# Summing runs of ten edges on VectorE before the products of sums on TensorE

## The reference, cut to what matters

```python
msg_in = concat([h[src], h[dst], edge_attr])          # 206250 x 160, h = relu(layernorm(x))
messages = silu(msg_in @ W1 + b1) @ W2 + b2           # 64 wide
att_logits = silu(msg_in @ Wa1 + ba1) @ Wa2 + ba2     # one number per edge
att = softmax(att_logits, axis=0)                     # over all edges
aggregated = segment_sum(messages * att, dst, 6250)
x + silu(concat([h, aggregated]) @ Wu1 + bu1) @ Wu2 + bu2
```

## Time and profile before

| | |
|---|---|
| timed runs, median | 2107.86 us |
| profiled execution, span | 2482.0 us |
| mean granted TensorE clock | 0.668 |
| busy: GpSimd | 1529.9 us (62%) |
| busy: TensorE matmul | 1101.1 us (44%) |
| busy: VectorE | 1086.6 us (44%) |
| busy: ScalarE | 919.5 us (37%) |
| mean DMA share of 16 engines | 18.5% + 17.2% in the two large queues |

### The profile page before, as it was taken

How to read it: one execution, slowest core, us unless ns; L and a number is a source line. 1 busy time by engine, 2 the same in 40 slices (tenths; PEclk the granted TensorE clock), 3 DMA queues, 4 the chain that set the end, 5 groups by cost and what they waited for, 6 DMA issues and landing times.

```text
span 2482.0 us, 21022 instructions
## 1 busy us (share of the span) xinstructions
PE 1101.1 (44%) x6767; PEld 963.4 (39%) x6767; DVE 1086.6 (44%) x2367; ACT 919.5 (37%) x1107; POOL 1529.9 (62%) x1628
## 2 busy tenths in 40 slices
PE   4334444444444444444444444444444444444447
PEld 3223343444333333444333334343433333444444
DVE  4344444444444444444444444444444444444445
ACT  3333333334333333334333333343433333333433
POOL 4666666666666666666666666666666666666650
PEclk8566666666666666666666666666666666666766
DMA  7433333333333333333333333333333333333321
GB/s 202 106 90 90 90 89 88 92 91 95 98 93 88 90 88 88 90 93 90 99 95 89 89 90 89 87 94 89 98 95 91 89 90 90 87 93 90 95 65 27
DMA packets 101990, 228.43 MB, mean 92 GB/s; under 512 B 45184, under 2 KB 65460, under 8 KB 91636
## 3 DMA queue, kind: packets, MB, share of 16 engines
q1 hardware_dynamic: 47588, 120.63, 18.5%
q0 software_dynamic: 51584, 105.75, 17.2%
q10 hardware_dynamic: 2704, 0.66, 0.1%
HBM read 218.91 MB, written 8.00 MB: 91 GB/s over the span
## 4 chain that ended last, share of the span: by engine, by line
issue 48%; PE 33%; DVE 9%; another core or an unknown queue 7%; ACT 1%; SPq 1%; DVEq 0%; DMA 0%; ACTq 0%
PE bank L622 20%; PE bank L636 11%; DVE hot L865 2%; DVE v L902 2%; DVE bank L912 1%; DVE prod L895 1%; PE bank L732 1%; PE bank L722 0%; DVE lgb L921 0%; DVEq L875 0%; ACT comb L492 0%; PE bank L584 0%; ACT s L524 0%; PE bank L655 0%
## 5 line engine op out<-in xcount | busy, mean ns | idle before, releaser
L404 POOL DMA_INDIRECT p_rows<-p_tab,src_all x1612 | 1521.9, 944 | 872.3 <-issue 464.7
L622 PE MATMUL bank<-q_win,comb 128*128 128x128 f32 x3224 | 723.7, 369 | 981.9 <-issue 963.8
L622 PEld LDWEIGHTS bank<-q_win,comb 128*128 128x128 f32 x3224 | 643.9, 279 | 1099.1 <-issue 1095.4
L492 ACT ACTIVATE comb<-dst_b,row_of 96x1024 f32<-96x1024 int32 (+1 forms) x162 | 219.0, 1352 | 1336.6 <-PE bank L622 1227.8
L911 DVE TENSOR_TENSOR bank<-bank,p_rows 128x128 f32<-128x128 f32 x80 | 23.9, 299 | 1205.5 <-remote 672.6
L636 PE MATMUL bank<-hot,v 128*65 128x96 f32 x3200 | 320.1, 252 | 344.7 <-issue 274.8
L636 PEld LDWEIGHTS bank<-hot,v 128*65 128x65 f32 x3200 | 282.7, 141 | 342.1 <-issue 264.5
L912 DVE TENSOR_TENSOR bank<-bank,p_rows 128x512 f32<-128x512 f32 (+1 forms) x403 | 266.5, 666 | 71.7 <-PE bank L622 38.6
L524 ACT ACTIVATE s<-bank 128x512 f32<-128x512 f32 x403 | 232.1, 589 | 108.7 <-DVE bank L912 83.8
L498 ACT ACTIVATE comb<-comb,ones 96x1024 f32<-96x1024 f32 (+1 forms) x162 | 218.9, 1351 | 2.7
L865 DVE TENSOR_TENSOR hot<-bank,rel 128x960 f32<-128x960 f32 x162 | 178.3, 1139 | 0.0
(11 more groups left out here) (108 smaller groups left out, 304.0 us busy)
## 6 DMA issues: line engine op xcount, KB each, us to landing
dst_b<-dst_row SPq DMA_DIRECT2D x80, 960.0 KB
p_rows<-p_tab,src_all POOLq DMA_INDIRECT x1612
comb<-efT SPq DMA_DIRECT2D x80, 320.0 KB
q_win<-q_tab SPq DMA_DIRECT2D x81, 48.0 KB
p_tab<-s SPq DMA_DIRECT2D x12, 256.0 KB
q_tab<-s SPq DMA_DIRECT2D x12, 256.0 KB
out<-s SPq DMA_DIRECT2D x6, 256.0 KB, 2.3
x_sb<-x SPq DMA_DIRECT2D x2, 512.0 KB, 5.1
```

The costliest lines, as they stand in the source:

```text
L404: pool.indirect_dma_start(p_rows[:, a, t * H2:(t + 1) * H2], None, p_tab, bass.IndirectOffsetOnAxis(src_all[:, g * TG + t:g * TG + t + 1], ...
L492: nc.scalar.activation(comb[0:WIN, a, c0:c1], dst_b[:, c0:c1], ACT.Abs, bias=row_of[0:WIN, bass.ds(g, 1)]).then_inc(abs_ok, 1)
L622: last = nc.tensor.matmul(ps_z[q][:, (t % TQ) * H2:(t % TQ + 1) * H2], comb[:, a, t * P:(t + 1) * P], q_win[:, a, :], start=True, stop=True)
```

## The change

The host lays the edges out differently: in a group, partition p now holds 20 consecutive edges instead of each 128th. Ten consecutive edges of one partition are a run (RUNS = 2 per group and partition; six edges in the last group). As edges are sorted by receiver, a run is taken to have at most two receivers, the first edge's and the last edge's. worst_fit checks this and keeps in first_run which edges have the receiver of their run's first edge.

Per group, VectorE splits the weights in two (w_run: those of first_run, and the others), multiplies s by each (the first product overwrites the logits' half of s2, the second goes to v), and adds up each over the ten edges of a run into run_sum: 4 columns of 65. One-hots are only needed for the first and last edge of each run, 4 tiles of 96. TensorE then has 4 products instead of 20. They stand behind all five quarters of the next z. The last group does the same, and its total weight is computed ahead of its sums.

```diff
+        first_run = sb("first_run", [P, C // P])
+        fits = sb("fits", [P, C // P])
+        hot = sb("hot", [P, SEGS * WIN])
+        w_run = sb("w_run", [P, 2, TG])
+        run_sum = sb("run_sum", [P, SEGS, U1])
...
             def sums(g):
-                pe.wait_ge(v_ok, g + 1)
-                pe.wait_ge(hot_ok, 2 * g + 2)
+                pe.wait_ge(hot_ok, g + 1)
                 wait(pe, acc_ok, g)
+                pe.wait_ge(run_ok, 2 * g + 2)
...
-                for t in range(T):
-                    last = nc.tensor.matmul(ps_part[0:U1, 0:WIN], v[:, t, :], hot[:, t * WIN:(t + 1) * WIN], start=(t == 0), stop=(t == T - 1))
+                for i in range(SEGS):
+                    last = nc.tensor.matmul(ps_part[0:U1, 0:WIN], run_sum[:, i, :], hot[:, i * WIN:(i + 1) * WIN], start=(i == 0), stop=(i == SEGS - 1))
                 last.then_inc(part_done, 1)
...
-                for q in [q for q in (0,) if q in quarters]:
-                    zmm(nxt, 1 - a, q)
-                for q in [q for q in (1, 2) if q in quarters]:
+                for q in quarters:
                     zmm(nxt, 1 - a, q)
                 if late:
                     sums(g - 1)
-                for q in [q for q in (3, 4) if q in quarters]:
-                    zmm(nxt, 1 - a, q)
...
+                for lo, hi, n in ((0, LAST * TG, TG // RUNS), (LAST * TG, C // P, TL // RUNS)):
+                    of_run = rel[:, lo:hi].rearrange("p (r t) -> p r t", t=n)
+                    for keep, end in ((first_run, 0), (fits, n - 1)):
+                        nc.vector.tensor_tensor(keep[:, lo:hi].rearrange("p (r t) -> p r t", t=n), of_run,
+                                                of_run[:, :, end:end + 1].broadcast_to([P, (hi - lo) // n, n]), ALU.is_equal).then_inc(run_fit, 1)
+                dve.wait_ge(run_fit, 4)
+                chain(nc.vector.tensor_tensor(fits[:], fits[:], first_run[:], ALU.max))
+                chain(nc.vector.tensor_reduce(bad[:, 0:1], fits[:], AX.X, ALU.min))
...
+            def one_hots(g):
+                n = tiles(g) // RUNS
+                nc.vector.tensor_tensor(hot[:].rearrange("p (r k n) -> p r k n", r=RUNS, k=2),
+                                        iota_c[:, 0:WIN].unsqueeze(1).unsqueeze(1).broadcast_to([P, RUNS, 2, WIN]),
+                                        runs(rel, g)[:, :, 0::n - 1].unsqueeze(3).broadcast_to([P, RUNS, 2, WIN]), ALU.is_equal).then_inc(hot_ok, 1)
...
+            def segment_sums(g, a):
+                T = tiles(g)
+                n = T // RUNS
+                here = slice(g * TG, g * TG + T)
+                att = s2[:, a, 0:T, U1:2 * U1]
+                nc.vector.tensor_tensor(w_run[:, 0, 0:T], ps_w[:, 0:T], first_run[:, here], ALU.mult).then_inc(w_run_ok, 1)
+                nc.vector.scalar_tensor_tensor(w_run[:, 1, 0:T], first_run[:, here], 0.5, ps_w[:, 0:T], ALU.is_lt, ALU.mult).then_inc(w_run_ok, 1)
+                for k, weighed in ((0, att), (1, v[:, 0:T, :])):
+                    dve.wait_ge(w_run_ok, 2 * g + 1 + k)
+                    nc.vector.tensor_tensor(weighed, s2[:, a, 0:T, 0:U1], w_run[:, k, 0:T].unsqueeze(2).broadcast_to([P, T, U1]), ALU.mult).then_inc(v_ok, 1)
+                for k, weighed in ((0, att), (1, v[:, 0:T, :])):
+                    dve.wait_ge(v_ok, 2 * g + 1 + k)
+                    nc.vector.tensor_reduce(run_sum[:, k::2, :], weighed.rearrange("p (r t) u -> p r u t", r=RUNS), AX.X, ALU.add).then_inc(run_ok, 1)
```

More of the change, by code:

```diff
@@ L56, in build @@
     RING = 6
+    RUNS = 2
+    SEGS = 2 * RUNS
     ACT_ODD = 6
     assert NT == NB * NBT + 1 and NT == UB * UT + 1 and NG % 2 == 1 and NB == 12
-    assert 0 <= DUP < P and TL % TQ == 0 and TL > 2 * TQ and src.shape == (P, C // P)
+    assert 0 <= DUP < P and TL % TQ == 0 and TL > 2 * TQ and TG % RUNS == 0 and TL % RUNS == 0 and src.shape == (P, C // P)
     assert H2 == P and 2 * D == P and U == D and DE * TQ == P
@@ L257, in tiles, with runs @@
             return TL if is_last(g) else TG
+        def runs(t, g):
+            return t[:, g * TG:g * TG + tiles(g)].rearrange("p (r t) -> p r t", r=RUNS)
         def per(a, g, n):
@@ L388, in _ @@
             nc.gpsimd.affine_select(out=mask[:], in_=mask[:], compare_op=ALU.is_gt, fill=1.0,
-                                    base=DUP, pattern=[[-P, TL]], channel_multiplier=-1).then_inc(const_ok, 1)
+                                    base=DUP, pattern=[[-1, TL]], channel_multiplier=-TL).then_inc(const_ok, 1)
             rows_stored(pool, NB + 1)
@@ L664, in _ @@
                 own_part(b)
[L665 to L674, removed]
+            pe.wait_ge(zp_ok, 1)
+            nc.tensor.matmul(ps_zall, ones[:], zp[:], start=True, stop=True).then_inc(zall_done, 1)
+            sums(LAST)
             pe.wait_ge(flag_ok, 1)
@@ L683, in group_any @@
                     for q in range(T // TQ):
-                        wait(pe, g_zok, g * NQ + q - 1)
+                        wait(pe, g_th, g * NQ + q - 1)
                         pe.sem_inc(turn, 1)
@@ L852, in worst_fit @@
                 chain(nc.vector.tensor_scalar(bad[:, 0:1], bad[:, 0:1], float(1 - WIN), None, ALU.add))
-                nc.vector.scalar_tensor_tensor(bad[:, 2:3], bad[:, 1:2], -1.0, bad[:, 0:1], ALU.mult, ALU.max).then_inc(bad_ok, 1)
+                chain(nc.vector.scalar_tensor_tensor(bad[:, 2:3], bad[:, 1:2], -1.0, bad[:, 0:1], ALU.mult, ALU.max))
+                for lo, hi, n in ((0, LAST * TG, TG // RUNS), (LAST * TG, C // P, TL // RUNS)):
[6 more added lines that the diff above has]
+                chain(nc.vector.tensor_reduce(bad[:, 0:1], fits[:], AX.X, ALU.min))
+                chain(nc.vector.tensor_scalar(bad[:, 0:1], bad[:, 0:1], -1.0, 1.0, ALU.mult, ALU.add))
+                nc.vector.tensor_tensor(bad[:, 2:3], bad[:, 2:3], bad[:, 0:1], ALU.max).then_inc(bad_ok, 1)
             def set_flag():
@@ L950, in weighted @@
                 dve.wait_ge(w_ok, 2 * g + 2)
-                weigh(T, a, a).then_inc(v_ok, 1)
+                nc.vector.tensor_reduce(wsum[:, a:a + 1], ps_w[:, 0:T], AX.X, ALU.add)
+                segment_sums(g, a)
             def group(g, a):
@@ L1022, in _ @@
             add_part(LAST - 1, 1, node_before)
-            one_hots(LAST, 0)
+            one_hots(LAST)
             dve.wait_ge(ref_ok, 2 * LAST)
@@ L1028, in _ @@
             dve.wait_ge(wm_ok, 1)
-            nc.vector.tensor_tensor(v[:, 0:TL, :], s2[:, 0, 0:TL, 0:U1], ps_w[:, 0:TL].unsqueeze(2).broadcast_to([P, TL, U1]), ALU.mult).then_inc(v_ok, 1)
-            one_hots(LAST, 1)
             nc.vector.tensor_reduce(wsum[:, 0:1], ps_w[:, 0:TL], AX.X, ALU.add).then_inc(ws_ok, 1)
@@ L1142 @@
     last = -(-(N_EDGES - full) // (4 * P)) * 4 * P
-    edges = np.concatenate([np.arange(full), np.arange(N_EDGES - last, N_EDGES)])
+    edges = np.concatenate([np.arange(full).reshape(-1, P, EDGE_TILES).transpose(0, 2, 1).reshape(-1),
+                            np.arange(N_EDGES - last, N_EDGES).reshape(P, -1).T.reshape(-1)])
     src, dst, ef = (np.ascontiguousarray(inputs[n])[edges] for n in ("src", "dst", "edge_attr_32"))
```

23 lines of the change are left out of this document (8 added, 15 removed).

## The result

| | us, median | lowest to highest |
|---|---|---|
| kernel before | 2106.89 | 2094.85 to 2108.01 |
| changed kernel | 2210.94 | 2207.96 to 2213.2 |

The ratio is 1.0507, 95% interval 1.0476 to 1.0538: 104 us more. The prediction was 2200 us, range 2112 to 2315.

The account below looks back on a forecast made before the run. The prediction took GpSimd's unbroken row of gathers, 1.248 us each, as the bound. From 2107.9 us it added 84 for held gathers, 2 for the fit check and 5 for the tail: 2199, say 2200 us, range 2112 to 2315.

Parts of the forecast that it names:

- The bound: GpSimd: timed runs are one unbroken row of 1612 gathers at 1.248 us with head and tail, 2095.5 us.
- TensorE, fewer products and their place: 0: TensorE: 16 of 20 sum products fewer per group, the rest behind all of z, change the time by 0.
- Gathers held by the products: +84: GpSimd: two products with both inputs in SBUF hold gathers, 1.05 us a group, 84 us (34 to 134).
- the single gather at 71.30: Set-up, earlier trace: gather starting inside L831, an operation with both inputs in SBUF, took 1.95 us instead of 0.94.
- The even phase: Gather starts taken as even between 0 and 1.25 us into the first product: 1.05 us lost a group.
- VectorE: +3.15 us a group, hidden: VectorE: 15.9 us a group, 18.9 with reductions of double length, hidden under 24.96 us of gathers.
- Fit check: +2: Set-up: three added operations of some 1600 elements with both inputs in SBUF hold gathers once, +2 us.
- Tail: +5, up to +10: Last groups, where VectorE sets the pace: +3.5 and +1.5 us, +10 with reductions of double length.
- (1): Rival: a gather waits for both products, 2.30 us a group, 184 us, giving 2299 us; chance 0.22.
- (2): Rival: no contention that counts, the long gather being something else, 2113 to 2118 us; chance 0.10.
- (3): Rival: faster, as timed runs wait for TensorE like the profiled one; put at 1900 us; chance 0.06.
- (4): Rival: runs of ten edges with three nodes send all groups to the slow branch, several times the time; chance 0.01.

Follow-up runs that it names:

- order-only kernel: Kernel before with the last group's sums moved behind all five quarters of the next z: 2104.64 us, ratio 0.9995; in the condition of 2482, ratio 1.0185.
- w_sb: Kernel before with the softmax weights in SBUF instead of PSUM: 2200.91 us, ratio 1.0466; in the condition of 2482, 2488.01 us, ratio 1.0021.

## Why the prediction came out right, step by step

**The bound.** Right: one row of gathers at 1.248 us, and in the timed runs nothing else. Leaving out 393 gathers took 486 us off, 490 by that step. The order-only kernel shows the three parts at 2107: first gather at 46.1 us, a row of 2012.1, and 48.4 behind the last start, where the prediction had 40.0, 2011.8 and 43.7. Where it was wrong is the reading of the profiled execution. That its slow TensorE stretch stays out of the timed runs held for the runs forecast, but the profiling was not the reason: there is a condition in which every run takes about 2482 us, and in it GpSimd waits for VectorE and the row of gathers is not the bound.

**TensorE, fewer products and their place: 0.** Right for the time. For the place it is shown by the ratio 0.9995; fewer products alone were not run, but the other terms below leave nothing for them. The products saved are less than they look. In the run of the kernel before with w_sb, which has the old products and order in the same condition, z took 300 ns a matmul; in the changed kernel 424. The first row is of w_sb's page, the second of its cores, the third of the cores of the changed kernel.

```profile
L622 PE MATMUL bank<-q_win,comb 128*128 128x128 f32 x3224 | 454.2, 300 | 318.6 <-ACT s L524 312.2
```

```profile
core 0: 2196.7 us, clock 0.670
```

```profile
core 0: 2209.6 us, clock 0.544
```

z and sums together were busy 454.2 + 447.0 = 901 us there and 792.3 + 122.6 = 915 us in the changed kernel: four fifths of the sums' matmuls are gone, and TensorE is not less busy. It got less clock: a burst of 8 records of z takes 1.16 us there at 1028.13 and 2.08 here at 413.96, and 13% of z's records start at the lower clock, 1.2 GHz, there and 90% here. Not all of this comes with the fewer products. In the order-only kernel, with every old product and a mean clock of 0.673, 50% do and z is busy 644.6 us; with its sums, 448.6, that is 1093 us. So the saving depends on which kernel one compares with.

**Gathers held by the products: +84.** Right in kind, 9 us short in size. In the two profiles of the changed kernel the gathers held by products lose 93.3 and 93.1 us. The timed difference to the kernel with w_run in PSUM is 92.6 us; from first to last gather start it is 2106.2 against 2016.8 us in the two profiles taken beside each other, 89.4, a little less, in part because single gathers of the set-up lose 1.5 us more in the second. The rule from the single gather at 71.30, held at 0.13 us behind its start until the instruction ends, gives an end 0.944 - 0.13 = 0.81 us behind the product's, and that is what 159 + 76 gathers show. (The row is not quite the only long one of 1612: the first gather takes 1.10 us in each of these traces, which changes nothing.)

The size was off since the phase, the place in the product at which a gather starts, is not spread evenly. In 73 groups a gather starts up to 0.4 us into the first product and loses 0.99 us or more, and the next 0.2. A likely reason, not tested, is that VectorE's work of a group begins at a gather's landing, so that the products keep their distance from the gathers. The even phase gave 1.05 us a group, the measured one is 1.2. That the forecast came this close is in part luck: nobody had worked out the phase, and in the kernel with w_sb one product alone, with the gather at 0.1 to 0.2 us, lost 1.2 us.

The Trainium skill, SBUF — State Buffer, section Who interferes with whom, says that a VectorE instruction with two SBUF inputs contends with a GpSimd instruction that reads SBUF: this case's trace agrees, 80 + 79 gathers. It also tells of a probe in which tensor_tensor did not stall a DMA's descriptors. GpSimd's row gathers, which read their row numbers from SBUF, do stall: 92.6 us of 2212 come and go with w_run's place. Which part of a gather is held, the reading or the making of descriptors, no run here shows.

**VectorE: +3.15 us a group, hidden.** The cover held (no GpSimd wait), the size failed: the reductions took 2.43 and 2.54 us, not 1.49. VectorE's busy time is 1259.26 us in 1860, or 17.7 us in a group of 26.2, between the value taken, 15.9, and the allowance of double length, 18.9. The row answers to the earlier trace rows:

```profile
240.00:2100.00 1860.00, 816.42 (x3426) 700.80 (x3425) 1259.26 (x2280) 793.40 (x925) 1426.33 (x1424) 0.53 0.40 102
```

The same page of the Trainium skill, in its passage on the DMA port swizzle, has 16-byte lines and a cost for each move to a new one. The runs agree in direction, with 2.43 against 1.49 us for the same 1300 elements.

**Fit check: +2.** Right. The three gathers beside L860 and L863 lose 1.8 and 2.3 us in the two profiles of the changed kernel and 2.5 with w_run in PSUM. The row of gathers with w_run in PSUM is 2016.8 us, that of the order-only kernel 2012.1. Of these 4.7 us 2.5 are the fit check's, and 1.1 more are a gather beside the old computation of rel, which lost 1.65 us in the one and 0.59 in the other by where it fell.

**Tail: +5, up to +10.** It came out at +9: from the last gather's start to the end 57.5 us in the changed kernel and 57.2 with w_run in PSUM, against 48.4 in the order-only kernel. Two things were missed. The four reductions take 3.1 us more than at the price of a dense one. And TensorE's last sums now start only behind the last reduction, at 2174.05, so that VectorE stands idle 3.60 us before the last update of acc, against 1.07 in the order-only kernel; the prediction had no term for that. First the changed kernel's tail, then the order-only kernel's:

```profile
2154.92 2.54 DVE L929 TENSOR_REDUCE run_sum<-s 128x130 f32<-128x1300 f32 x1
2157.37 2.43 DVE L929 TENSOR_REDUCE run_sum<-v 128x130 f32<-128x1300 f32 x1
2159.72 0.69 DVE L939 TENSOR_TENSOR bank<-bank,p_rows 128x512 f32<-128x512 f32 x1
...
2162.40 0.69 DVE L939 TENSOR_TENSOR bank<-bank,p_rows 128x512 f32<-128x512 f32 x1
...
2170.90 1.57 DVE L929 TENSOR_REDUCE run_sum<-s 128x130 f32<-128x780 f32 x1
2172.39 1.52 DVE L929 TENSOR_REDUCE run_sum<-v 128x130 f32<-128x780 f32 x1
...
2178.06 0.31 DVE L1131 SCALAR_TENSOR_TENSOR acc<-acc,fade,bank 65x96 f32 x1 [3.60 <-issue]
```

```profile
2060.33 0.69 DVE L910 TENSOR_TENSOR bank<-bank,p_rows 128x512 f32<-128x512 f32 x1
...
2063.00 0.69 DVE L910 TENSOR_TENSOR bank<-bank,p_rows 128x512 f32<-128x512 f32 x1
...
2073.87 0.31 DVE L1104 SCALAR_TENSOR_TENSOR acc<-acc,fade,bank 65x96 f32 x1 [1.07 <-issue]
```

The last gather starts at 2152.14 and at 2058.22. The last addition of rows comes 10.3 us behind it against 4.8, and from there to the last update of acc 15.7 us go by against 10.9; behind it the order-only kernel is 1.2 us longer.

**The sum.** 84 + 2 + 5 = 91 were forecast. 93 + 2 + 9 = 104 us are found, 104 and 105 were timed. The products' term was short by 9 and the tail's by 4; the fit check's held. Two slips in the prediction change nothing: GpSimd's longest wait in the earlier trace rows is 6.8 us and not 5.5, and its chances add up to 0.99.

**The rivals.** (1) fell: a gather gets through between the two products, which follow each other without a pause (414.95 above), and with pieces the loss shrinks. (2) fell with 168 long gathers; its sum, 2113 to 2118, describes the kernel with w_run in PSUM, 2119.84. (3) is out in the condition of 2107: the time followed the count of gathers. In the condition of 2482 GpSimd does wait for VectorE's addition, which waits for z. But the one version of the change that was tried there was 7.7% slower and not faster. (4) did not occur: the sums leave 8 records a group, 648 in 81.

**What stays open.** What puts the chip into the condition of 2482 was not found, nor was the changed kernel itself run in it. Why w_run in PSUM loses 7.7% there, of which the order alone explains 1.85, was not taken apart; that VectorE's 5 us more in each group delay the next addition is a guess. How much of z's lower clock comes with fewer products, beyond what the order alone brings, was not run alone either.

## What to carry to other kernels

When GpSimd's gathers set the pace, count the VectorE instructions whose two tensor inputs both lie in SBUF: each TENSOR_TENSOR of this kind held the gather that started in it until it ended. Put one input in PSUM, even a tiny one, or cut the instruction in pieces; both were tried, and gave 93 and 69 us of 2212 back. And price work taken off an engine by what ends last: here TensorE lost 2576 of the 3224 records of its sums, and the time gained nothing by it.

## What the hardware showed that was not expected

- A gather beside a VectorE product with both inputs in SBUF ends 0.80 to 0.83 us after the product, wherever in it it began. The first product of a group makes 1.93 us or more of 0.94 for the most part.
- One such product of 1300 elements cost 4.7% in the kernel before, about what two did in the changed kernel, by the phase of the gathers.
- A reduction of 1300 elements that reads with a step of 65 elements took 2.43 us, with 130 elements 2.54, dense 1.49. A product that writes with a step of 20 elements took 2.82 us, dense 1.50.
- The same kernel took 2107 us on one chip and 2482 on another, each steady within 1%. In the slower condition TensorE's instructions often come 0.7 to 2.8 us apart with no wait shown: some 880 times in the first profile of the kernel before, of which 256 while GpSimd itself stood waiting, against 2 times in the order-only kernel at 2107.
- With four fifths of the sums' matmuls gone and the rest behind z, the granted clock fell from 0.670 to 0.544, and z's matmul went from 300 to 424 ns.
